# Layer 3 of a four-layer image network: softmax weights used unscaled, their sums made on TensorE, the division on VectorE

## The chip, the cores and the metric

The kernel runs on one core of one Trainium2 chip, as one program for four layers. The metric is the device time in microseconds (us). Three runs of the kernel before gave 3361.9, 3371.34 and 3377.48 us; their median is 3371.34 us.

## The reference, cut to what matters

The input is a batch of 8 images of 32 x 32 tokens with 256 channels. Each of the four layers adds its output to its input. Only layer 3 changes, a windowed attention with 8 heads of 32 channels and a window of 7 x 7 tokens:

```
qkv  = silu(x @ w_qkv.T)                       # q, k get an RMS norm and a scale per head; v does not
wp   = silu(x @ w_wp.T + b_wp)                 # gives width and sharp, one each per token and head
scores = einsum('blhd,blwhd->blhw', q, k_win) * D ** -0.5
soft = sigmoid((width - rel_dist) * sharp)
scores = scores - (1 - soft) * 10000.0
attn = softmax(scores)                         # over the 49 places of the window
out  = einsum('blhw,blwhd->blhd', attn, v_win)
out  = rms_norm(out, w_on)                     # over the 256 channels of a token
return silu((out + v) @ w_out.T)
```

The softmax divides each row of exponentials by its sum. The division can be made on the weights, before they meet the values, or on the weighted sum of the values, which is what the change moves.

## The kernel before, in words

A layer is a block in which each engine has its own program, written out by hand; engines meet at semaphores (`wait_ge`, `then_inc`). No planner orders anything: what stands in the loops is the order on each engine, and each engine takes its instructions strictly in that order.

An image is cut into 64 tiles of 4 x 4 tokens. The keys of a tile are the 10 x 10 tokens around it. A step N handles 4 tiles, so 16 steps make an image and 128 steps the layer; in the text a step's number n within its image runs from 0 to 15, and b is the image. In a tile 16 tokens x 8 heads fill the 128 partitions, and 100 keys lie along the row, so a step's weights are 128 x 400 numbers (`logits`).

The work of one step, in class `Tiles`:

- TensorE `scores` (L1762, with a mask added by L1754), for steps N and N + 1 together when N is even.
- VectorE `add_and_low` (L1802): adds the soft mask, and takes the least value of a row, for both steps at the even one.
- ScalarE `exps` (L1822): four activations of 128 x 100, each with its own row's least value as bias, each followed by a read of its accumulated sum.
- VectorE `invert` (L1808): the reciprocal of the 128 x 4 sums, one step later.
- GpSimd `scale` (L1829): multiplies 128 x 400 weights by these, one step later.
- TensorE `turn` (L1774): transposes the weights, two steps after the scores.
- VectorE `copy_turned` (L1814): copies them out of PSUM.
- TensorE `weigh` (L1789): 32 small matmuls (4 tiles x 8 heads), three steps after the scores. Each fills 32 partitions by 16 columns, so four lie side by side in the array. Each matmul of fp32 data in the code is two in the trace.

The weighted sums of 8 steps (half an image) gather in two PSUM banks; `copy_out` on ScalarE (L2679, at n = 10 and at n = 2 of the next image) takes them to `OT` and squares them (L2682). TensorE averages the squares (`out_mean`, L2409, after the other work of n = 11 and of n = 3), ScalarE makes the root (`root_of_out`, L2690, L2692), VectorE scales (`finish`, L2519, L2522), and the output projection (L301 with `w_out`) follows.

Beside this, the steps of image b also prepare image b + 1: projections at n = 4 to 10 (L2366, L309, L301, L2349), each read by ScalarE's tanh (L2617) and VectorE's product (L2494) through a ring of two PSUM banks (`ring`), so that a projection waits until the one two places before it has been taken; squares, means and roots of queries and keys at n = 10 to 15 (L2641, L2643, L2391, L2657, L2659), and VectorE's scaling of queries and keys by them (L2531, L2512). The scores of the next image wait for the last scaled key. GpSimd makes the soft mask's arguments at n = 4 to 10 (`soft_args`, L2786), ScalarE its tanh (`soften`, L2627). The group norm of the next image takes VectorE (L386 to L395), TensorE (L400), GpSimd and ScalarE at n = 0 to 3.

Of the kernel before, what the change touches and what calls it, by code (L numbers as in the profile page):

```python
# [13 lines left out]
P = 128  # L14
# [1827 lines left out]

def edge(t):
    return 0 if t == 0 else 2 if t == BANDS - 1 else 1
# [352 lines left out]
def layer3_order():  # L2197

    order = [("gn", 0)] + [unit_name(u, -1) for n in range(4, 11) for u in layer3_units(n) if u[0] != "out"]
    order += [("mean", 0, j) for j in range(8)]  # L2200
    for b in range(B + 1):
        for n in range(STEPS):
            if b < B:
                order += {0: [("vT", b, 0, 0)], 1: [("vT", b, 0, 1), ("vT", b, 1, 0)], 2: [("vT", b, 1, 1)]}.get(n, [])
            if n == 2 and b + 1 < B:
                order.append(("gn", b + 1))
            order += [name for name in (unit_name(u, b) for u in layer3_units(n)) if name is not None]
            if b + 1 < B:
                order += [("mean", b + 1, j) for j in range(*MEANS_AT.get(n, (0, 0)))]
            if n == 3 and b > 0:  # L2210
                order.append(("om", b - 1, 1))
            if n == 11 and b < B:
                order.append(("om", b, 0))
    return order


def layer3(nc, A, x, out, vimg):
    with ExitStack() as ctx:
# [29 lines left out]
        OT = L.sb("OT", [P, HALVES, T])  # L2248
# [8 lines left out]
        w = Tiles(L, keys, IMAGE, vimg, 5)  # L2257
# [16 lines left out]
        with nc.Block() as block:  # L2274
# [66 lines left out]
            def _(pe):  # L2341
# [12 lines left out]
                def unit(name):  # L2354
# [21 lines left out]
                    elif kind == "k":  # L2376
                        g, half = name[2] % 2, name[2] // 2
                        pe.wait_ge(xn_ready, 4 * (b + 1))
                        ring.may_fill(pe, name)
                        project(nc, ring.region(name), wqkv, xn, HALVES + g, half * BANK, (half + 1) * BANK).then_inc(ring.filled(name), 1)  # L2380
                    else:
                        half, m = name[2], name[3]
                        pe.wait_ge(z_ready, 4 * b + 2 * half + 2)
                        ring.may_fill(pe, name)
                        project(nc, ring.region(name), wo, OT, m, half * BANK, (half + 1) * BANK).then_inc(ring.filled(name), 1)
# [36 lines left out]
                for N in range(B * STEPS + 10):  # L2422
# [19 lines left out]
                    if 3 <= N < B * STEPS + 3:  # L2442
                        w.weigh(nc, pe, N - 3)
                    for u in layer3_units(n):
                        if unit_name(u, b) is not None:
                            unit(unit_name(u, b))
# [3 lines left out]
                    if n == 3 and b > 0:  # L2450
                        out_mean(b - 1, 1)
                    if n == 11 and b < B:
                        out_mean(b, 0)

            @block.vector
            def _(dve):
# [57 lines left out]

                def finish(b, half, g):
                    s = slice(half * BANK, (half + 1) * BANK)
                    H = 2 * b + half
                    dve.wait_ge(or_ready, H + 1)
                    vstep(dve, nc.vector.scalar_tensor_tensor(OT[:, g, s], OT[:, g, s], w_on[:, g:g + 1], orec[:, :], ALU.mult,  # L2519
                                                              ALU.mult))  # L2520
                    ring.is_taken(dve, ("vT", b, half, g))
                    nc.vector.tensor_tensor(OT[:, g, s], OT[:, g, s], VT[:, H % 3, g, :], ALU.add).then_inc(z_ready, 1)  # L2522
# [18 lines left out]
                nc.vector.memset(all_mean[:, :], 1.0 / C)  # L2541
                nc.vector.memset(keys[0][:, :, :], 0.0)
# [23 lines left out]
                for N in range(B * STEPS + 10):  # L2566
# [30 lines left out]
                    if n == 12 and b < B:  # L2597
# [4 lines left out]
            def _(act):  # L2602
# [66 lines left out]
                def copy_out(b, half):  # L2669
                    H = 2 * b + half  # L2670
                    act.wait_ge(w.weighed, STEPS // 2 * (H + 1))
# [4 lines left out]
                    s = slice(half * BANK, (half + 1) * BANK)  # L2676
                    for g in range(HALVES):
                        bank = PS[:, (4 + g) * BANK:(5 + g) * BANK]
                        nc.scalar.activation(OT[:, g, s], bank, ACT.Copy).then_inc(w.o_copied, 1)  # L2679
                    for g in range(HALVES):  # L2680
                        act.wait_ge(w.o_copied, 2 * H + g + 1)
                        nc.scalar.activation(osq[:, g, :], OT[:, g, s], ACT.Square).then_inc(o_squared, 1)  # L2682
# [42 lines left out]
                for N in range(B * STEPS + 10):  # L2725
                    b, n = step_of(N)
                    if n == 4:
                        nc.scalar.preload_act_table_set("exp_and_others")
# [11 lines left out]
                    if n == 2 and b > 0:  # L2740
                        copy_out(b - 1, 1)
                    if n == 2 and b + 1 < B:
                        norm.root(nc, act, b + 1)
                    if n == 3 and b > 0:
                        root_of_out(b - 1, 1)
# [6 lines left out]
                    if n == 10 and b < B:  # L2752
                        copy_out(b, 0)
# [4 lines left out]
                    if n == 11 and b < B:  # L2758
# [10 lines left out]
            def _(pool):  # L2769
# [124 lines left out]
```

## Time and profile before

| | |
|---|---|
| median of three runs | 3371.34 us |
| the profiled execution | 3381.97 us |
| its span in the profile | 3380.1 us |
| its granted TensorE clock, mean | 0.946 |
| layer 3, first exponentials to the end | about 2660 to 3380 us |

The profile is of one execution. A row of a group of instructions has how often it ran, its busy time, the mean of one, and the idle time of its engine ahead of it with what ended it. A row of the order in time has start, length, engine, line and operation. Successive operations of one engine overlap by a little, so that a chain of them is measured from start to start. Line numbers are those of the kernel before.

### The profile page before, as it was taken

The numbers are of one execution on the slowest core, as the hardware profiler recorded it, in microseconds if no ns is written. First come the engines' busy times: TensorE is split into PE (matmuls) and PEld (weight loads), VectorE is DVE, ScalarE is ACT, GpSimd is POOL, SyncE is SP. The second block draws the span as 40 slices with busy tenths as digits, with TensorE's granted clock in tenths as the row PEclk, the third lists the DMA queues.
The fourth block names the chain that finished last, engine by engine and source line by source line (L and its number), as shares of the span: only waits on it lengthen the run. The fifth ranks groups of instructions, "written<-read, shape, count | busy, mean of one in ns | idle before, by whom it ended". The sixth has DMA issues, their size and how long they took to land. (4 is left out here: it accounts for less than half of the span.)

```text
span 3380.1 us, 103119 instructions
## 1 busy us (share of the span) xinstructions
PE 3018.3 (89%) x43264; PEld 1668.5 (49%) x43264; DVE 2138.1 (63%) x5157; ACT 1995.5 (59%) x4348; POOL 1134.3 (34%) x1444
## 2 busy tenths in 40 slices
PE   6999999999985899999999977999995788888886
PEld 2333333333322565555565645667663555555553
DVE  5787778878753676767667643554553466665654
ACT  2667676766662556455556533555552677777774
POOL 3443433434311221222222201222221455554643
PEclk9999999999986999999999988999996899999997
DMA  6877778687763233333333214545444233333332
GB/s 200 163 170 153 172 171 179 143 187 162 145 142 114 62 86 81 73 89 86 86 69 81 67 47 148 159 150 169 149 148 145 69 92 115 117 115 113 117 103 76
DMA packets 299756, 414.89 MB, mean 123 GB/s; under 512 B 39424, under 2 KB 256288, under 8 KB 278304
## 3 DMA queue, kind: packets, MB, share of 16 engines
q1 hardware_dynamic: 275664, 272.46, 27.1%
q0 software_dynamic: 18432, 134.23, 19.9%
q8 instruction: 344, 5.64, 0.7%
q10 hardware_dynamic: 5200, 1.62, 0.2%
q14 instruction: 116, 0.95, 0.1%
HBM read 219.67 MB, written 53.81 MB: 81 GB/s over the span
## 5 line engine op out<-in xcount | busy, mean ns | idle before, releaser
L734 DVE TENSOR_TENSOR l_probs<-l_psum,l_decay 128x1024 f32<-128x1024 f32 x512 | 598.6, 1219 | 164.7 <-PE l_psum L630 154.0
L782 ACT ACTIVATE l_sizes<-l_probs 128x2048 f32<-128x2048 f32 x256 | 487.1, 1908 | 303.2 <-DVE l_probs L734 292.1
L1822 ACT ACTIVATE l_logits<-l_logits,l_low 128x100 f32<-128x100 f32 x1024 | 372.7, 366 | 203.4 <-DVE l_low L1802 202.7
L1829 POOL TENSOR_TENSOR l_logits<-l_logits,l_inv 128x400 f32<-128x400 f32 x256 | 242.9, 950 | 679.9 <-DVE l_inv L1808 679.2
L630 PE MATMUL l_psum<-l_qk 32*128 32x512 f32 x2048 | 340.2, 645 | 7.9 <-POOL l_qk L868 4.2
L883 POOL DMA_DIRECT2D l_sizes<-l_sizes x128 | 111.5, 871 | 549.3 <-ACT l_sizes L782 537.3
L1645 POOL TENSOR_TENSOR l_E<-l_E,l_causal 128x1024 f32<-128x1024 f32 x64 | 153.0, 2390 | 381.6 <-DVE l_x_act L1343 224.6
L645 PE MATMUL l_psum<-l_probs,l_V 128*32 128x512 f32 x2048 | 270.6, 600 | 1.7 <-DVE l_probs L734 1.6
L1814 DVE COPY l_PT<-l_psum 100x512 f32<-100x512 f32 x256 | 173.0, 676 | 114.4 <-PE l_psum L1774 113.9
L301 PE MATMUL l_psum<-l_xT,l_w_up 128*128 128x512 f32 x512 | 231.3, 606 | 9.1 <-DVE l_row_var L1401 9.0
L1789 PE MATMUL l_psum<-l_PT,l_V_windows 100*32 100x16 f32 x16384 | 202.6, 187 | 34.9 <-issue 22.6
L2786 POOL TENSOR_SCALAR l_soft<-l_dist,l_sharp,l_border 128x100 f32<-128x100 f32 x512 | 225.4, 459 | 0.1
L630 PEld LDWEIGHTS l_psum<-l_qk 32*128 32x128 f32 x2048 | 100.7, 184 | 248.8 <-issue 190.3
L1789 PEld LDWEIGHTS l_psum<-l_PT,l_V_windows 100*32 100x32 f32 x16384 | 174.3, 112 | 87.0 <-issue 84.2
L1774 PE MATMUL l_psum<-l_ident,l_logits 128*100 128x128 f32 x1024 | 166.2, 287 | 33.4 <-POOL l_logits L1829 30.5
L1822 ACT ACTIVATION_READ_ACCUMULATOR l_logits<-l_logits,l_low 128x1 f32 x1024 | 191.9, 187 | 0.0
L1774 PEld LDWEIGHTS l_psum<-l_ident,l_logits 128*100 128x100 f32 x1024 | 118.1, 134 | 103.3 <-POOL l_logits L1829 50.1
L301 PEld LDWEIGHTS l_psum<-l_xT,l_w_up 128*128 128x128 f32 x512 | 97.0, 195 | 121.1 <-issue 121.1
L1500 ACT ACTIVATE l_E<-l_E,l_tok_vals 128x128 f32<-128x128 f32 x512 | 155.9, 393 | 0.0
L1802 DVE CUSTOM_DVE_ANT_0 l_logits<-l_psum,l_soft 128x100 f32<-128x100 f32 x512 | 98.5, 256 | 86.5 <-issue 67.0
L1762 PE MATMUL l_psum<-l_keys,l_q_blocks 64*32 64x100 f32 x8192 | 141.4, 259 | 10.4 <-issue 8.1
L654 PE MATMUL l_psum<-l_sizes,l_ones 128*32 128x512 f32 x1024 | 137.5, 609 | 11.8 <-DMA l_sizes<-l_sizes 11.8
(246 smaller groups left out, 5883.8 us busy)
## 6 DMA issues: line engine op xcount, KB each, us to landing
l_sizes<-l_sizes POOLq DMA_DIRECT2D x128, 1024.0 KB, 7.6
l_V_windows<-v_image SPq DMA_DIRECT2D x512, 100.0 KB
l_V_windows<-v_padded SPq DMA_DIRECT2D x512, 100.0 KB
l_E<-rows_c SPq DMA_DIRECT2D x64, 512.0 KB, 5.8
l_xT<-y SPq DMA_DIRECT2D x24, 1024.0 KB, 5.3
y<-l_res SPq DMA_DIRECT2D x32, 512.0 KB, 3.1
l_e_everywhere<-rows_e SPq DMA_DIRECT2D x112, 128.0 KB, 5.6
l_xT<-x SPq DMA_DIRECT2D x8, 1024.0 KB, 11.3
```

Of the source, the lines that this page charges most:

```text
L301: i = nc.tensor.matmul(out, w[:, k, m * P:(m + 1) * P], act[:, k, n0:n1], start=(k == 0), stop=(k == tiles - 1))
L630: i = nc.tensor.matmul(out[:, a * BANK:(a + 1) * BANK], qk[r:r + HD, g, 1, J * P:(J + 1) * P], qk[r:r + HD, g, 0, m * BANK:(m + 1) * BANK] ...
L645: i = nc.tensor.matmul(PS[a * HD:(a + 1) * HD, 6 * BANK:7 * BANK], V[:, J, h * HD:(h + 1) * HD], probs[:, N % 2, a, :], start=(J == 0), st ...
L734: nc.vector.tensor_tensor(probs[:, N % 2, 2 * p:2 * p + 2, :], ring.region(name).rearrange("p (a n) -> p a n", a=2), decay[:, h:h + 2, s0: ...
L782: nc.scalar.activation(sizes[:, slot(N), :, :], probs[:, N % 2, :, :], ACT.Abs).then_inc(sized, 1)
L1500: i = nc.scalar.activation(E[:, N % 3, h, :], E[:, N % 3, h, :], ACT.Exp, scale=-1.0, bias=vals[:, u % 2, c0:c0 + 1])
L1774: m = nc.tensor.transpose(self.ps[0:NKEY, c0:c0 + P], self.logits[:, N % 4, i, :], self.ident[:, :])
L1789: m = nc.tensor.matmul(out[:, r0:r0 + TILE, tc * TILE:(tc + 1) * TILE], self.v[0:NKEY, N % self.slots, i, h * HD:(h + 1) * HD], self.pt[0: ...
L1814: nc.vector.tensor_copy(self.pt[0:NKEY, N % 2, :], self.ps[0:NKEY, (2 + N % 2) * BANK:(3 + N % 2) * BANK]).then_inc(self.pt_ready, 1)
L1822: nc.scalar.activation(e, e, ACT.Exp, scale=-1.0, bias=self.low[:, N % 4, i:i + 1], accum_out=self.total[:, N % 4, i:i + 1]).then_inc(self ...
L1829: nc.gpsimd.tensor_tensor(p, p, self.inv[:, N % 4, :].unsqueeze(2).to_broadcast([P, STEP, NKEY]), ALU.mult).then_inc(self.p_ready, 1)
L2786: m = nc.gpsimd.tensor_scalar(soft[:, M % SOFTS, i * NKEY:(i + 1) * NKEY], dist[:, :], sharp[:, b % 2, t:t + 1], border[:, b % 2, t:t + 1] ...
```

## The change

Layer 3 uses a subclass of `Tiles`, `SummedTiles`. GpSimd now subtracts the least value from the scores ahead of the exponential (`lower`), ScalarE makes one activation of 128 x 400 instead of four with sums (`exps`), and nothing is scaled. TensorE turns and weighs the bare exponentials, and behind the 32 matmuls of a step makes 8 more with a weight of ones, 64 columns each, which give the row's sums in the place of the weighted values. VectorE divides (`divide`) for two steps at a time, at odd steps: a reciprocal of 128 x 256 from PSUM and a product of 128 x 256. The two banks are used by turns of two steps. `OT` has two buffers.

Moved with it: the average of the output's squares (`out_mean`) from behind the work of n = 3 and 11 to the middle of n = 4 and 12; `out_squares`, which is `copy_out` without the copies, by one step; the root of the first half from n = 11 to 12, that of the second half from n = 3 to the head of n = 4; `finish` of the first half from n = 12 to 13. Layer 2 stays as it was.

```diff
+class SummedTiles(Tiles):
+    def bank(self, R):
+        return (4 + R % 2) * BANK
+
+    def weigh(self, nc, pe, N):
+        R = N // 2
+        pe.wait_ge(self.pt_ready, N + 1)
...
+        if N % 2 == 0 and R >= 2:
+            pe.wait_ge(self.o_copied, R - 1)
...
+        for g in range(HALVES):
+            for a in range(4):
+                p = self.place(N, 4 * g + a)
...
+                m = nc.tensor.matmul(out[:, N % 2 * STEP:(N % 2 + 1) * STEP], self.ones[0:NKEY, :], of[:, :, p],
+                                     start=True, stop=True)
+        m.then_inc(self.weighed, 1)
+
+    def exps(self, nc, act, N):
+        act.wait_ge(self.lowered, N + 1)
+        p = self.logits[:, N % 4, :, :]
+        nc.scalar.activation(p, p, ACT.Exp, scale=-1.0).then_inc(self.p_ready, 1)
+
+    def lower(self, nc, pool, N):
+        pool.wait_ge(self.l_ready, STEP * (N + 1))
+        p = self.logits[:, N % 4, :, :]
+        nc.gpsimd.tensor_tensor(p, p, self.low[:, N % 4, :].unsqueeze(2).to_broadcast([P, STEP, NKEY]),
+                                ALU.subtract).then_inc(self.lowered, 1)
...
+                def divide(R):
+                    c0 = w.bank(R)
+                    s = slice(R % 8 * P, (R % 8 + 1) * P)
+                    dve.wait_ge(w.weighed, 2 * (R + 1))
...
+                    vstep(dve, nc.vector.reciprocal(w.share[:, R % 2, :], PS[:, c0 + 2 * P:c0 + 4 * P]))
+                    nc.vector.tensor_tensor(OT[R // 8 % 2][:, :, s], PS[:, c0:c0 + 2 * P].rearrange("p (g t) -> p g t", g=HALVES),
+                                            w.share[:, R % 2, :].rearrange("p (g t) -> p g t", g=HALVES), ALU.mult).then_inc(w.o_copied, 1)
...
-                    if 1 <= N < B * STEPS + 1:
-                        w.invert(nc, dve, N - 1)
                     if 2 <= N < B * STEPS + 2:
                         w.copy_turned(nc, dve, N - 2)
+                    if n % 2 == 1 and 4 < N < B * STEPS + 5:
+                        divide(N // 2 - 2)
...
-                    if n == 12 and b < B:
+                    if n == 13 and b < B:
                         finish(b, 0, 0)
                         finish(b, 0, 1)
...
-                for N in range(B * STEPS + 1):
+                for N in range(B * STEPS):
                     b, n = step_of(N)
-                    if N > 0:
-                        w.scale(nc, pool, N - 1)
+                    w.lower(nc, pool, N)
```

The change moves instructions on four engines. Two places of it follow, of the kernel before and of the changed kernel apart; names begin with `l_`, `ISA` is `add_and_low`, and the line numbers of the changed kernel are its own.

TensorE around n = 11 and 12 before, from the turn of n = 11 to that of n = 13 (`l_O_square` are the squares of the output, `l_square` those of queries and keys):

```order
 L1774 MATMUL l_psum<-l_ident,l_logits 100x128 x4
 L1789 MATMUL l_psum<-l_PT,l_V_windows 32x4x4 x32
 L2409 MATMUL l_psum<-l_O_square,l_all_mean 128x512 x2
 L1754 MATMUL l_psum<-l_outside,l_pick 32x400 x8
 L1762 MATMUL l_psum<-l_keys,l_q_blocks 32x100 x32
 L1774 MATMUL l_psum<-l_ident,l_logits 100x128 x4
 L1789 MATMUL l_psum<-l_PT,l_V_windows 32x4x4 x32
 L2391 MATMUL l_psum<-l_square,l_head_mean 128x512 x2
 L1774 MATMUL l_psum<-l_ident,l_logits 100x128 x4
```

The same stretch of TensorE in the changed kernel:

```order
 L1774 MATMUL l_psum<-l_ident,l_logits 100x128 x4
 L1868 MATMUL l_psum<-l_PT,l_V_windows 32x4x4 x32
 L1876 MATMUL l_psum<-l_PT,l_ones 32x4x4x4 x8
 L1754 MATMUL l_psum<-l_outside,l_pick 32x400 x8
 L1762 MATMUL l_psum<-l_keys,l_q_blocks 32x100 x32
 L1774 MATMUL l_psum<-l_ident,l_logits 100x128 x4
 L1868 MATMUL l_psum<-l_PT,l_V_windows 32x4x4 x32
 L1876 MATMUL l_psum<-l_PT,l_ones 32x4x4x4 x8
 L2460 MATMUL l_psum<-l_O_square,l_all_mean 128x512 x2
 L2442 MATMUL l_psum<-l_square,l_head_mean 128x512 x2
 L1774 MATMUL l_psum<-l_ident,l_logits 100x128 x4
```

The average of the output's squares moved behind the scores of n = 12 and 13 and directly ahead of the means, and each weighing has 8 sums behind it.

VectorE from the end of n = 12 to the first scores of n = 14 before (`l_O_rec` is the root for the output, `l_q_blocks` the scaled queries):

```order
 L1808 RECIPROCAL l_inv<-l_total 128x4
 L1814 COPY l_PT<-l_psum 100x512
 L2519 SCALAR_TENSOR_TENSOR l_OT<-l_OT,l_w_on,l_O_rec 128x512
 L2522 TENSOR_TENSOR l_OT<-l_OT,l_VT 128x512
 L2519 SCALAR_TENSOR_TENSOR l_OT<-l_OT,l_w_on,l_O_rec 128x512
 L2522 TENSOR_TENSOR l_OT<-l_OT,l_VT 128x512
 L1808 RECIPROCAL l_inv<-l_total 128x4
 L1814 COPY l_PT<-l_psum 100x512
 L2531 SCALAR_TENSOR_TENSOR l_q_blocks<-l_silu_q,l_pair,l_rec 128x32x16 x2
 L1802 ISA l_logits,l_low<-l_psum,l_soft 128x100
```

The same stretch of VectorE in the changed kernel:

```order
 L1814 COPY l_PT<-l_psum 100x512 x2
 L2572 RECIPROCAL l_share<-l_psum 128x256
 L2573 TENSOR_TENSOR l_OT<-l_psum,l_share 128x2x128
 L2592 SCALAR_TENSOR_TENSOR l_q_blocks<-l_silu_q,l_pair,l_rec 128x32x16 x2
 L2581 SCALAR_TENSOR_TENSOR l_OT<-l_OT,l_w_on,l_O_rec 128x512
 L2583 TENSOR_TENSOR l_OT<-l_OT,l_VT 128x512
 L2581 SCALAR_TENSOR_TENSOR l_OT<-l_OT,l_w_on,l_O_rec 128x512
 L2583 TENSOR_TENSOR l_OT<-l_OT,l_VT 128x512
 L1802 ISA l_logits,l_low<-l_psum,l_soft 128x100
```

The four operations of `finish` moved from ahead of the copy of n = 13 to behind the queries of that step, and a division of two steps stands between that copy and the queries; the small reciprocals are gone.

## Rows read from the trace of the kernel before

**Rows 1.** Image 2, n to 10, then 11 on: length; PE, PEld, DVE, ACT, POOL busy; clock.
```profile
2829.20:2893.20 64.00, 57.68 (x1393) 40.80 (x1394) 39.79 (x161) 42.23 (x142) 41.66 (x85) 0.97 0.37 105
2893.20:2917.90 24.70, 19.44 (x507) 10.54 (x505) 15.67 (x55) 24.14 (x67) 6.68 (x6) 1.00 0.43 134
```

**Rows 2.** Chain of waits, image 2: start, length, engine and line.
```profile
2857.61 5.84 POOL l_soft L2786 x12
...
2894.01 1.08 ACT l_OT L2679 x2
...
2902.55 1.54 ACT l_logits L1822 x8
```

**Rows 3.** TensorE in order of time, image 2.
```profile
2838.37 0.28 PE L400 MATMUL l_psum<-l_gn_mean_var,l_group_mean 128*128 128x4 f32 x2
...
2842.16 0.72 PE L1789 MATMUL l_psum<-l_PT,l_V_windows 100*32 100x16 f32 x64 [0.70 <-ACT l_OT L2679]
2843.11 3.64 PE L2409 MATMUL l_psum<-l_O_square,l_all_mean 128*128 128x512 f32 x4 [0.22 <-ACT l_O_square L2682]
...
2848.96 0.75 PE L2366 MATMUL l_psum<-l_xn,l_w_wp 128*32 128x64 f32 x36
2850.93 0.64 PE L2366 MATMUL l_psum<-l_xn,l_w_wp 128*32 128x64 f32 x28 [1.22 <-issue]
...
2866.81 1.95 PE L301 MATMUL l_psum<-l_OT,l_w_out 128*128 128x512 f32 x4 [1.05 <-DVE l_V L2494]
```

**Rows 4.** Groups by line, 2655 to 3350 us.
```profile
L1822 ACT ACTIVATE l_logits<-l_logits,l_low 128x100 f32<-128x100 f32 x512 | 185.8, 365 | 21.9 <-DVE l_low L1802 21.4 <-issue 0.3
L1829 POOL TENSOR_TENSOR l_logits<-l_logits,l_inv 128x400 f32<-128x400 f32 x128 | 133.6, 1045 | 306.5 <-DVE l_inv L1808 305.9
L2627 ACT ACTIVATE l_soft<-l_soft 128x400 f32<-128x400 f32 x122 | 62.4, 534 | 61.8 <-POOL l_soft L2786 61.3
L2366 PE MATMUL l_psum<-l_xn,l_w_wp 128*32 128x64 f32 x448 | 9.5, 224 | 9.5 <-issue 9.5
```

**Rows 5.** VectorE, whole span, groups by line and shape.
```profile
L734 DVE TENSOR_TENSOR l_probs<-l_psum,l_decay 128x1024 f32<-128x1024 f32 x512 | 598.6, 1219 | 164.7 <-PE l_psum L630 154.0 <-ACT l_sizes L782 10.3
L1808 DVE RECIPROCAL l_inv<-l_total 128x4 f32<-128x4 f32 x256 | 44.0, 172 | 4.4 <-ACT l_logits L1822 4.4
L1396 DVE TENSOR_TENSOR l_row_norm<-l_psum,l_row_norm 128x128 f32<-128x128 f32 x64 | 18.7, 292 | 2.2
L1366 DVE COPY l_carry<-l_row_m 128x1 f32<-128x1 f32 x16 | 2.5, 154 | 0.6
```

**Rows 6.** VectorE in order of time, image 2.
```profile
2837.60 0.16 DVE L395 TENSOR_TENSOR l_gn_mean_var<-l_gn_mean_var,l_gn_mean 128x2 f32<-128x2 f32 x1
...
2894.14 0.69 DVE L2494 SCALAR_TENSOR_TENSOR l_silu_q<-l_tanh,l_psum 128x512 f32<-128x512 f32 x1 [1.10 <-ACT l_tanh L2617]
...
2902.14 0.75 DVE L2519 SCALAR_TENSOR_TENSOR l_OT<-l_OT,l_w_on,l_O_rec 128x512 f32<-128x512 f32 x1 [0.17 <-ACT l_O_rec L2692]
...
2904.31 0.69 DVE L2522 TENSOR_TENSOR l_OT<-l_OT,l_VT 128x512 f32<-128x512 f32 x1
...
2905.01 0.66 DVE L1814 COPY l_PT<-l_psum 100x512 f32<-100x512 f32 x1
2905.90 1.41 DVE L2531 SCALAR_TENSOR_TENSOR l_q_blocks<-l_silu_q,l_pair,l_rec 128x512 f32<-128x512 f32 x2 [0.23 <-ACT l_rec L2659]
2908.87 0.26 DVE L1802 CUSTOM_DVE_ANT_0 l_logits<-l_psum,l_soft 128x100 f32<-128x100 f32 x1 [1.55 <-issue]
...
2910.33 0.17 DVE L1808 RECIPROCAL l_inv<-l_total 128x4 f32<-128x4 f32 x1
...
2917.11 0.75 DVE L2512 SCALAR_TENSOR_TENSOR l_keys<-l_keys,l_w_qk,l_rec 128x512 f32<-128x512 f32 x1 [0.49 <-ACT l_rec L2659]
```

**Rows 7.** TensorE in order of time, last image.
```profile
3288.84 3.75 PE L2409 MATMUL l_psum<-l_O_square,l_all_mean 128*128 128x512 f32 x4 [0.97 <-issue]
...
3298.55 1.09 PE L1774 MATMUL l_psum<-l_ident,l_logits 128*100 128x128 f32 x4 [3.13 <-POOL l_logits L1829]
```

More of the change, by code:

```diff
@@ L1840, in gather, with __init__ @@
             sp.dma_start(self.v[0:NKEY, N % self.slots, i, :], src).then_inc(self.v_loaded[N % self.slots], 16)
+class SummedTiles(Tiles):
+    def __init__(self, L, keys, side, vimg, slots):
+        Tiles.__init__(self, L, keys, side, vimg, slots)
+        self.ones = L.sb("ones", [P, 32])
+        self.share = L.sb("share", [P, 2, 2 * P])
+        self.lowered = self.inv_ready
+    def bank(self, R):
[3 more added lines that the diff above has]
+        pe.wait_ge(self.pt_ready, N + 1)
+        pe.wait_ge(self.v_loaded[N % self.slots], 16 * STEP * (N // self.slots + 1))
+        if N % 2 == 0 and R >= 2:
+            pe.wait_ge(self.o_copied, R - 1)
+        c0 = self.bank(R)
+        for i in range(STEP):
+            tc = N % 2 * STEP + i
+            for g in range(HALVES):
+                for a in range(4):
+                    h = 4 * g + a
+                    out = self.ps[a * HD:(a + 1) * HD, c0 + g * P:c0 + (g + 1) * P].rearrange("p (r c) -> p r c", c=SIDE)
+                    nc.tensor.matmul(out[:, :, tc * TILE:(tc + 1) * TILE], self.v[0:NKEY, N % self.slots, i, h * HD:(h + 1) * HD],
+                                     self.pt[0:NKEY, N % 2, i * P + self.place(N, h) * 16:i * P + (self.place(N, h) + 1) * 16],
+                                     start=True, stop=True)
+        for g in range(HALVES):
+            for a in range(4):
+                p = self.place(N, 4 * g + a)
+                out = self.ps[a * HD:(a + 1) * HD, c0 + (2 + g) * P:c0 + (3 + g) * P].rearrange("p (r t c) -> p t r c", r=TILE, c=TILE)
+                of = self.pt[0:NKEY, N % 2, :].rearrange("p (i h r c) -> p i h r c", i=STEP, h=NH, c=TILE)
+                m = nc.tensor.matmul(out[:, N % 2 * STEP:(N % 2 + 1) * STEP], self.ones[0:NKEY, :], of[:, :, p],
+                                     start=True, stop=True)
+        m.then_inc(self.weighed, 1)
[8 more added lines that the diff above has]
+                                ALU.subtract).then_inc(self.lowered, 1)
@@ L2206, in layer3_order @@
                 order.append(("gn", b + 1))
+            if n == 4 and b > 0:
+                order.append(("om", b - 1, 1))
+            if n == 12 and b < B:
+                order.append(("om", b, 0))
             order += [name for name in (unit_name(u, b) for u in layer3_units(n)) if name is not None]
@@ L2247, in layer3 @@
         VT = L.sb("VT", [P, 3, HALVES, BANK])
-        OT = L.sb("OT", [P, HALVES, T])
+        OT = [L.sb(f"OT{s}", [P, HALVES, T]) for s in range(2)]
         osq = L.sb("O_square", [P, HALVES, BANK])
@@ L2256, in layer3 @@
         norm = Groups(L, xT)
-        w = Tiles(L, keys, IMAGE, vimg, 5)
+        w = SummedTiles(L, keys, IMAGE, vimg, 5)
         wp_in = square[:, 0:2, 0:P]
@@ L2675, in copy_out @@
                         ring.is_full(act, ("om", (H - 1) // 2, (H - 1) % 2))
-                    s = slice(half * BANK, (half + 1) * BANK)
                     for g in range(HALVES):
[L2678 to L2682, printed above, removed]
+                        nc.scalar.activation(osq[:, g, :], OT[b % 2][:, g, half * BANK:(half + 1) * BANK],
+                                             ACT.Square).then_inc(o_squared, 1)
                 def root_of_out(b, half):
```

41 lines of the change are left out of this document (20 added, 21 removed).

## The prediction, made before the changed kernel had run

> **What bounds the kernel now.** I read the stretches first, then the chain of waits, then TensorE and VectorE in order of time. Image 2 stands for the six images with work of a neighbour on both sides. It takes 88.7 us from its scores to those of image 3, in two parts with different limits [rows 1]. In n = 0 to 10 TensorE is busy for 57.7 of 64.0 us and no other engine for more than 42.2: the projections of the next image run there, and what TensorE is given more is paid in full. In n = 11 to 15 ScalarE is busy for 24.1 of 24.7 us, TensorE for 19.4, VectorE for 15.7. The chain agrees: exponentials, squares and roots of ScalarE end last there, the eight records of a step's exponentials taking 1.54 us each time [rows 2]. GpSimd comes into the chain once an image, at n = 5, where 5.84 us of mask arguments stand behind a scaling that waited for VectorE's small reciprocal [rows 2].
>
> **ScalarE.** Four activations and four reads fall to one activation of 128 x 400. The nearest row is the mask's tanh of that shape, 534 ns [rows 4]. So 1.54 becomes 0.53, 16 times an image, and the two copies of half an image (1.08 [rows 2]) go twice. That is 16.2 + 2.2 = 18.4 us of ScalarE an image, 5 x 1.01 + 1.08 = 6.1 of it in n = 11 to 15. None of it is time of the kernel unless nothing else is late, and that is where VectorE comes in.
>
> **TensorE.** Eight sums a step are 16 records of 64 columns on 32 columns of the array. The row of that shape is the width and sharpness projection: 36 records in 0.75 us and 28 in 0.64, or 22 ns each with four side by side [rows 3]; 16 x 22 = 0.35 us a step. Bounds: 0.72 us for 64 records of 16 columns [rows 3] give 0.18; records that don't overlap at all, 16 x 224 ns [rows 4], give 3.6. I take 0.35, since shape and columns are the same. In n = 0 to 10 that is 11 x 0.35 = +3.9 us an image.
> Against it stand waits of TensorE in the same part [rows 3]. The weighing of step 0 waited 0.70 us for the copy out of the banks; two banks by turns take that away. The output's mean waited 0.22 for its squares, and took 3.64 us at the lower clock level (1.2 GHz), where the output projection's four records of the same shape took 1.95 at the higher (2.4 GHz); it now stands behind the scores of n = 4, the stretch has no gap, and I take the higher level: 1.7. The output projection waited 1.05 us behind a projection that ScalarE read late because of GpSimd's arguments; GpSimd's subtraction no longer waits for exponentials and small reciprocals, its arguments start sooner by as much, and that goes. Sum -3.7.
>
> **VectorE.** The 16 small reciprocals leave (0.17 us, some 0.09 from start to start). Eight times an image a division comes, at odd steps: a reciprocal of 128 x 256 and a product. The product is an ordinary operation: from 292 ns at 128 to 1219 at 1024 elements it grows by 1.03 ns an element, so 256 take 0.42 us [rows 5]. The reciprocal has one row, 172 ns for 4 elements, and its price an element hides in 172 minus a fixed part. If it streams like the product, 0.42 us: the lower bound. If all 172 ns belonged to the 4 elements, 43 ns each, it would be 11 us: the upper. Between: one element of a copy takes 154 ns [rows 5], so three more cost 18, 6 ns each; 256 take 0.15 + 1.54 = 1.7 us. With 134 ns as the fixed part (a PSUM copy of 512 in 0.66 us, less 512 x 1.03 [rows 6]) it is 9.5 ns each, 2.6 us. I take 1.7, from the row that differs by the fewest elements, and so d = 2.1 us a division; both ends stay for the range.
> The Trainium skill speaks against this change here: "VectorE: DVE Perf Modes", section "First, the fixed hardware budget", says that the reciprocal is an iterative divide with a repeat count of 8. Read as eight cycles an element at the page's 0.96 GHz that is an estimate of 2.3 us, and the sum below would come to some 3400. No row here has a reciprocal of more than 4 elements, so the trace neither shows nor refutes it.
>
> Where d lies. In n = 0 to 10 VectorE has room (39.8 of 64.0 us [rows 1]), and the projections' ring holds a product that is 2 us late. One place has little: at n = 1 the division stands ahead of the group norm's statistics, and TensorE's group mean now starts 0.6 us after their last operation has ended at 2837.76 [rows 3, 6]. TensorE itself comes there 0.7 us later (two steps' sums); VectorE comes 0.35 - 0.1 + 2.1 = 2.35 later, and with some 0.1 for the semaphore the wait is about +1.1. So n = 0 to 10 changes by 3.9 - 3.7 + 1.1 = +1.3.
>
> In n = 11 to 15 the order is what counts. From X, the end of the projections (2893.2): VectorE's last product starts at X + 0.94 [rows 6] and holds it to 1.55, copy 2.15, division 4.25; ScalarE squares two (1.1) to 5.35; TensorE, free from 4.4 (turn, weighing with sums, scores, turn, weighing), makes the output's mean and the first two means of queries, 1.9 each, then the turn of n = 11: X + 9.75. Only then can VectorE copy step 11, and from there it doesn't rest: copy 0.6, division 2.1, queries 1.3, the four operations of `finish` 2.8 (2902.14 to 2904.92), scores of n = 14 and 15 1.46 (2908.87 to 2910.33), copy 0.6, queries 1.3, one key 0.7, copy 0.6, division 2.1, three keys 2.2 [rows 6] = 15.8. The last key is done at X + 25.5. Before it started at 2917.11 and ended at X + 24.7: +0.8. So ScalarE's 6.1 us go to VectorE, which takes ScalarE's place.
>
> New waits. ScalarE's exponential waits for GpSimd's subtraction (0.85 us undisturbed; mean 1.05 with disturbed ones in [rows 4]) behind the mask's arguments of the step before; behind it stand the tanh of that step's projections. GpSimd is busy for 41.7 of 64 us, so I cost it at nothing; at even steps the exponential is ready 1.3 us after the first score instead of 0.3, while the ring's slack is a whole projection (1.95 [rows 3]). The weights are wanted only two steps later. VectorE's wait for the weighing is met, since the copy ahead of it waits for a later turn. The root of the second half now stands ahead of the exponential of n = 4 and waits for a mean in that step; it ended there before too. No DMA is moved.
>
> **The sum.** An inner image +1.3 + 0.8 = +2.1, six of them +12.6. Image 0 has the sums and divisions but no output of a neighbour whose waits go: +3. In the last image the output's mean (3.75 us at the lower clock) moves behind the scores of n = 4 and 5, and the turn that waited 3.13 us for GpSimd's scaling is free of it [rows 7]: -4 after the divisions. The tail has a division for two copies: +0.5. Together +12 on the profiled execution's 3382 us, 3394. That execution lies 10.6 us above the median of the runs; on the median the sum is 3383 us.
>
> **Rivals.**
> 1. The reciprocal streams (0.42 us, d = 0.85). The group mean then waits for nothing, n = 0 to 10 gives 3.9 - 3.7 = +0.2; the squares are done at X + 4.1, so TensorE's 4.4 decides, the turn ends at 8.8, VectorE's 15.8 fall to 13.3: X + 22.1, -2.6. Six images by -2.4, image 0 -1, the last -5: -20, 3351 us. For it: 172 ns for 4 is near the 154 of any small operation [rows 5].
> 2. The reciprocal is dear (9.5 ns, d = 3.0). The group mean waits 2.0, n = 0 to 10 gives +2.2; the squares are done at X + 6.25, the turn at 10.65, VectorE's chain is 17.6: X + 28.2, +3.5. Six by +5.7, image 0 +5, the last -3: +36, 3407 us. It makes the kernel slower from d = 2.4 on or so. The page's eight cycles would be a little less than this.
> 3. TensorE's sums are dear: the small matmuls already stop for 0.7 to 1.2 us with no releaser (1.22 in [rows 3]), and the change adds a seventh to TensorE's records. At 0.9 us a step instead of 0.35, 11 x 0.55 = 6 more an image, 8 images 48: 3430 us.
> That ScalarE gains nothing is not a rival but part of the forecast.
>
> **How the numbers follow.** Forecast 0.38, rival 1 0.32, rival 2 0.23, rival 3 0.07. A measurement of this kernel can tell about 0.5% from no change, that is 3354 to 3388. Errors of 2 us an image give each case some 12 us either way. Forecast (its own range 3368 to 3400): same 0.25, slower 0.13. Rival 1: faster 0.19, same 0.13. Rival 2: slower 0.20, same 0.03. Rival 3: slower 0.07. So faster 0.19, same 0.41, slower 0.40. The range 3342 to 3418 reaches into both main rivals and leaves out about 0.07 below and 0.11 above. A reciprocal at its upper bound of 11 us would be far outside.
>
> **What would show it.** The reciprocal's mean: 1.7 right, 0.4 rival 1, over 2.3 rival 2. The sums: 16 records within 0.35 us behind a weighing. In n = 11 to 15 VectorE should have no rest from the copy of step 11 to the last key, with ScalarE idle ahead of the exponential of n = 14. In n = 0 to 10 the three waits of [rows 3] should be gone, the mean of n = 4 at the higher clock level, and the group mean should wait for VectorE by about 1 us. Wrong would be: ScalarE still without rest at n = 12 to 15, TensorE's ring waiting for VectorE's products at n = 5 to 9, or GpSimd late with the subtraction at n = 5 to 7.

## The result, and the profile after

The changed kernel takes 3437.49 us in the median (3430.66 to 3446.47), the kernel before 3374.41 beside it: ratio 1.019, 95% interval 1.0146 to 1.0234. It is slower, by 1.5 to 2.3%, and lies 54 us above the forecast, beyond its range.

All traces of this study are read by one cut: the six images 1 to 6, from the first mask record of an image to the end of its last query projection (part A, n = 0 to 10) and from there to the next image (part B, n = 11 to 15). Before, A is 64.5 and B 24.5 us in the mean; after, 70.7 and 27.9. (The rows of image 2 end A 0.3 us earlier, where that projection's last record starts.) So an image is 9.6 us longer instead of 2.1, 57 us over six images; image 0 is 0.4 shorter (83.2 for 83.6), last image and tail 3.2 (102.0 for 105.2). Ahead of layer 3's first scores the code is the same, yet they start between 2650 and 2687 us in the profiled executions here (2658 before, 2669 after), and nothing here explains that; so the cut is sharper than the totals. Each kernel has one trace, though: how far A and B differ between executions of one kernel was not measured, and the six A of a trace lie 1 to 6 us apart.

Image 2 after, A and B (columns as in [rows 1]):

```profile
2850.00:2919.94 69.94, 62.34 (x1569) 44.30 (x1570) 49.18 (x160) 28.54 (x57) 44.54 (x86) 0.95 0.33 94
2919.94:2952.27 32.33, 22.61 (x587) 12.89 (x585) 21.01 (x56) 20.23 (x35) 5.61 (x5) 0.89 0.34 107
```

ScalarE fell from 42.2 to 28.5 and from 24.1 to 20.2 us: 17.6 an image where 18.4 were foretold, but 3.9 of it in B instead of 6.1, since one more pair of roots falls into B. In B no engine is busy for more than 22.6 of 32.3 us: there the time is waiting. The groups of layer 3 after, by line (busy, mean ns | idle before them):

```profile
L1890 POOL TENSOR_TENSOR l_logits<-l_logits,l_low 128x400 f32<-128x400 f32 x128 | 124.0, 977 | 352.0 <-DVE l_low L1802 351.4
L2572 DVE RECIPROCAL l_share<-l_psum 128x256 f32<-128x256 f32 x64 | 111.7, 1746 | 0.0
...
L1884 ACT ACTIVATE l_logits<-l_logits 128x400 f32<-128x400 f32 x128 | 68.0, 532 | 182.5 <-POOL l_logits L1890 182.4
L1876 PE MATMUL l_psum<-l_PT,l_ones 100*32 100x64 f32 x2048 | 64.6, 230 | 20.9 <-issue 20.9
...
L2573 DVE TENSOR_TENSOR l_OT<-l_psum,l_share 128x256 f32<-128x256 f32 x64 | 27.2, 425 | 2.2
```

Three of these durations came as foretold: the reciprocal 1.75 us, its product 0.42, the exponential 0.53 [rows 4, 5]. The two idle times were not: ScalarE waits 182 us for GpSimd's subtraction, and TensorE stops 20.9 us among the sums with no releaser. TensorE in order of time, image 2 (idle time before a row in brackets):

```profile
2861.05 0.39 PE L400 MATMUL l_psum<-l_gn_mean_var,l_group_mean 128*128 128x4 f32 x2 [0.93 <-DVE l_gn_mean_var L395]
...
2869.10 1.98 PE L2460 MATMUL l_psum<-l_O_square,l_all_mean 128*128 128x512 f32 x4
...
2887.64 1.98 PE L301 MATMUL l_psum<-l_OT,l_w_out 128*128 128x512 f32 x4
...
2900.68 3.75 PE L301 MATMUL l_psum<-l_OT,l_w_out 128*128 128x512 f32 x4 [2.84 <-DVE l_silu_q L2545]
...
2925.47 0.31 PE L1876 MATMUL l_psum<-l_PT,l_ones 100*32 100x64 f32 x4
2929.75 0.64 PE L1876 MATMUL l_psum<-l_PT,l_ones 100*32 100x64 f32 x12 [3.97 <-issue]
2930.32 3.78 PE L2460 MATMUL l_psum<-l_O_square,l_all_mean 128*128 128x512 f32 x4
...
2935.91 0.60 PE L1774 MATMUL l_psum<-l_ident,l_logits 128*100 128x128 f32 x4
```

Against [rows 3]: the group mean waits, as foretold; the mean of n = 4 is at the higher clock level (1.98 for 3.64), as foretold. Of the four output projections of an image the second, which had waited 1.05 us, waits no longer, as foretold. But the third waits 2.84 us and then runs at the lower level (1.2 GHz, 3.75 us). Before, it was this row:

```profile
2876.91 1.95 PE L301 MATMUL l_psum<-l_OT,l_w_out 128*128 128x512 f32 x4 [0.17 <-DVE l_silu_q L2494]
```

Over six images the wait of the second fell from 1.1 to 0, that of the third rose from 0.2 to 2.2, and all four together rose from 1.6 to 2.7 us an image; only in image 2 did the third run at the lower level. And in the middle of one weighing's sums TensorE stands for 3.97 us; the mean of n = 12 behind it runs at the lower level, 3.78, and the turn of n = 11, on which VectorE's chain hangs, starts at X + 16.0 (X = 2919.94) instead of X + 9.15 (the prediction's X + 9.75, less the turn's 0.6). VectorE meanwhile:

```profile
2936.55 0.69 DVE L1814 COPY l_PT<-l_psum 100x512 f32<-100x512 f32 x1 [10.14 <-PE l_psum L1774]
...
2950.14 2.07 DVE L2563 SCALAR_TENSOR_TENSOR l_keys<-l_keys,l_w_qk,l_rec 128x512 f32<-128x512 f32 x3
```

From that copy to the last key it takes 15.66 us, foretold 15.8, with no rest but 10 us of idleness ahead of it.

**The stop.** A stop is here idle time of TensorE that no releaser ends. TensorE's loads from one stop to the next:

```profile
2923.29 0.72 PEld L1762 LDWEIGHTS l_psum<-l_keys,l_q_blocks 64*32 64x32 f32 x55 [1.50 <-issue]
2924.16 0.39 PEld L1774 LDWEIGHTS l_psum<-l_ident,l_logits 128*100 128x100 f32 x4 [0.15 <-issue]
2924.74 0.83 PEld L1868 LDWEIGHTS l_psum<-l_PT,l_V_windows 100*32 100x32 f32 x64 [0.18 <-issue]
2925.47 0.15 PEld L1876 LDWEIGHTS l_psum<-l_PT,l_ones 100*32 100x32 f32 x4
2929.75 0.40 PEld L1876 LDWEIGHTS l_psum<-l_PT,l_ones 100*32 100x32 f32 x12 [4.13 <-issue]
```

127 loads, as many matmuls and two waits: 256 records. Counted through the whole trace, nearly all long stops stand a multiple of 256 TensorE records apart (48 of the 57 over 0.7 us; before, 28 of 30). In the same 4 us the DMA queues show:

```profile
q1 hardware_dynamic: 530, 1.02, 64.9%
q8 instruction: 1, 0.02, 1.4%
```

One 16 KB packet of the queue "instruction" (it ran from 2927.36 to 2928.30), beside 1 MB of other transfers; TensorE went on 1.45 us after it. Of the stops at such a multiple every one over 0.7 us in the six images ends 1.2 to 1.6 us after such a packet. There are 103 such packets in the six images, and TensorE's 26,250 records are 102.5 times 256; before, 91 for 90.5. So TensorE waits for its program. In six images these stops are 41.3 us after and 16.0 before.
The Trainium skill ("Runtime: NRT & Kernel Launch", section "Instruction fetch mechanics") says that instructions come in 16 KiB blocks of 256 while the engine runs, the crossing mostly hidden. The trace agrees on the block; hidden it is not here, with 6.9 us an image.

**GpSimd.** GpSimd, then ScalarE, ahead of the third output projection:

```profile
2889.58 4.25 POOL L2844 TENSOR_SCALAR l_soft<-l_dist,l_sharp,l_border 128x100 f32<-128x100 f32 x8
2896.85 0.24 POOL L2832 TENSOR_SCALAR l_sharp<-l_args 128x64 f32<-128x64 f32 x1 [3.02 <-DMA l_args<-l_rec]
...
2897.90 0.85 POOL L1890 TENSOR_TENSOR l_logits<-l_logits,l_low 128x400 f32<-128x400 f32 x1
```

```profile
2898.79 0.54 ACT L1884 ACTIVATE l_logits<-l_logits 128x400 f32<-128x400 f32 x1 [4.38 <-POOL l_logits L1890]
2899.23 1.06 ACT L2679 ACTIVATE l_tanh<-l_psum 128x512 f32<-128x512 f32 x2
```

At n = 7 GpSimd waits for the DMA with the next image's width and sharpness. Before, a scaling stood behind that wait, wanted a step later:

```profile
2874.91 0.24 POOL L2774 TENSOR_SCALAR l_sharp<-l_args 128x64 f32<-128x64 f32 x1 [1.66 <-DMA l_args<-l_rec]
...
2875.98 0.86 POOL L1829 TENSOR_TENSOR l_logits<-l_logits,l_inv 128x400 f32<-128x400 f32 x1
```

Now the subtraction of n = 8 stands there, behind it the exponential, the tanh, VectorE's product, the projections' ring and TensorE.

### The profile page after: what moved, and what is told of

Same layout as the page of the kernel before. It is cut to its first block and busy times, and to the rows that moved or that the text cites. A ratio compares the mean times of both kernels' runs of the same rounds, so it can differ in the third digit from the quotient of the medians.

```text
span 3444.7 us, 106350 instructions
## 1 busy us (share of the span) xinstructions
PE 3053.7 (89%) x45312; PEld 1703.4 (49%) x45312; DVE 2255.3 (65%) x5158; ACT 1855.1 (54%) x3420; POOL 1132.6 (33%) x1444
## 5 line engine op out<-in xcount | busy, mean ns | idle before, releaser
L1822 ACT ACTIVATE l_logits<-l_logits,l_low 128x100 f32<-128x100 f32 x512 | 186.9, 366 | 182.9 <-DVE l_low L1802 182.8
L1890 POOL TENSOR_TENSOR l_logits<-l_logits,l_low 128x400 f32<-128x400 f32 x128 | 124.0, 977 | 352.0 <-DVE l_low L1802 351.4
L1829 POOL TENSOR_TENSOR l_logits<-l_logits,l_inv 128x400 f32<-128x400 f32 x128 | 109.1, 853 | 381.5 <-DVE l_inv L1808 379.1
L1884 ACT ACTIVATE l_logits<-l_logits 128x400 f32<-128x400 f32 x128 | 68.0, 532 | 182.5 <-POOL l_logits L1890 182.4
L1802 DVE CUSTOM_DVE_ANT_0 l_logits<-l_psum,l_bias 128x100 f32<-128x100 f32 x512 | 102.7, 257 | 71.3 <-PE l_psum L1762 71.3
L1387 DVE TENSOR_TENSOR l_faded<-l_state,l_tok_vals 128x264 f32<-128x264 f32 x48 | 37.2, 774 | 162.6 <-PE l_psum L1265 162.6
```

What stands on the lines that cost most here:

```text
L1822: nc.scalar.activation(e, e, ACT.Exp, scale=-1.0, bias=self.low[:, N % 4, i:i + 1], accum_out=self.total[:, N % 4, i:i + 1]).then_inc(self ...
L1890: nc.gpsimd.tensor_tensor(p, p, self.low[:, N % 4, :].unsqueeze(2).to_broadcast([P, STEP, NKEY]), ALU.subtract).then_inc(self.lowered, 1)
```

## The experiments

Times are medians, ratios go to the kernel before of the same runs; A and B are means over the six images of one trace. The traced execution lies up to 22 us above its kernel's median (run 3) and up to 18 us below it (run 1).

| kernel | median, ratio (interval) | A | B | A + B |
|---|---|---|---|---|
| before | 3374.4 to 3388.2 | 64.5 | 24.5 | 88.9 |
| changed | 3437.5, 1.019 (1.0146 to 1.0234) | 70.7 | 27.9 | 98.5 |
| 1 arguments behind step 8 | 3438.5, 1.0167 (1.0127 to 1.0206) | 67.9 | 28.1 | 96.1 |
| 2 sums in half as many | 3414.7, 1.0091 (1.0058 to 1.0124) | 67.8 | 25.8 | 93.6 |
| 3 no sums | 3423.0, 1.0122 (1.0076 to 1.0168) | 69.2 | 26.2 | 95.4 |
| 4 copy for reciprocal | 3412.2, 1.0083 (1.0053 to 1.0112) | 70.4 | 26.1 | 96.6 |
| 5 = 1 + 2 | 3393.0, 1.0036 (1.0009 to 1.0064) | 66.2 | 25.8 | 92.0 |
| 6 divisions moved | 3432.0, 1.0115 (1.0076 to 1.0154) | 69.4 | 27.6 | 97.0 |
| 7 all moves | 3401.7, 1.0059 (1.0025 to 1.0092) | 68.8 | 23.7 | 92.5 |
| 8 exponential alone | 3387.2, 1.0002 (0.9974 to 1.003) | 67.3 | 22.1 | 89.4 |
| 9 = 8, arguments moved | 3343.5, 0.9873 (0.9823 to 0.9922) | 62.9 | 21.2 | 84.1 |
| 10 = 7, finish spread | 3406.8, 1.0063 (1.0034 to 1.0092) | 70.2 | 23.7 | 93.9 |
| 11 sums in twice as many | 3470.0, 1.0254 (1.0208 to 1.0299) | 72.6 | 28.5 | 101.2 |
| 12 = 5, copy | 3351.1, 0.9895 (0.9855 to 0.9934) | 64.1 | 22.3 | 86.4 |
| 13 = 9, old division | 3404.0, 1.0085 (1.0053 to 1.0117) | 67.2 | 25.5 | 92.7 |
| 14 = 13, pairs | 3408.2, 1.0087 (1.0061 to 1.0114) | 67.3 | 26.2 | 93.5 |
| 15 = 3, arguments moved | 3400.3, 1.006 (1.0037 to 1.0084) | 65.4 | 26.3 | 91.6 |

**1.** GpSimd's arguments behind the subtraction of step 8.

```diff
                     w.lower(nc, pool, N)
+                    if b + 1 < B and n == 8:
+                        affine(b + 1)
...
-                        if n == 7:
-                            affine(b + 1)
```

> One line moved: GpSimd's three operations on the width and sharpness of the next image (and the wait for the DMA that brings them) stand behind its subtraction of step 8 instead of ahead of it. Theory G (ScalarE's exponential now waits for a GpSimd that stands still for those arguments: 3.0 us at n = 8 of image 2, then TensorE stops 2.7 us ahead of the output projection and runs its next 12 records at the lower clock): each of six images loses that stop, 2 us of it and about as much of low clock, so 3 to 4 us an image, 3415 to 3420 us, and the wait of the exponential of n = 8 falls from 4.4 to about 1 us. Theory I (TensorE stops for its instructions) and theory V (the division on VectorE) expect 3437 within 7.

GpSimd, then TensorE at the third and fourth output projection of image 2:

```profile
2884.61 0.85 POOL L1890 TENSOR_TENSOR l_logits<-l_logits,l_low 128x400 f32<-128x400 f32 x1 [2.09 <-DVE l_low L1802]
2885.43 0.24 POOL L2832 TENSOR_SCALAR l_sharp<-l_args 128x64 f32<-128x64 f32 x1
```

```profile
2887.38 1.96 PE L301 MATMUL l_psum<-l_OT,l_w_out 128*128 128x512 f32 x4
...
2894.87 1.96 PE L301 MATMUL l_psum<-l_OT,l_w_out 128*128 128x512 f32 x4 [0.56 <-DVE l_keys L2545]
```

The subtraction waits for VectorE alone, and the projection runs at once and at the higher level. TensorE's waits at the output projections fall from 2.7 to 0.8 us an image and A falls by 2.7, under the forecast: the exponential of n = 8 still waits 2.4 us in image 2, and the time at the lower clock level in A hardly falls (6.0 to 5.6). The total does not fall (3438.5 for 3437.5 us; the traced executions took 3420 and 3446), so this run alone does not show the price. Runs 2 and 5, 3 and 15, 8 and 9 differ by this edit too, and there the ratio falls: from 1.0091 to 1.0036, from 1.0122 to 1.006 and from 1.0002 to 0.9873.

**2.** Both halves of the heads in one matmul.

```diff
-        for g in range(HALVES):
-            for a in range(4):
-                p = self.place(N, 4 * g + a)
+        for a in range(4):
+            p = self.place(N, a)
...
```

> The sums of both halves of the heads come in one matmul of 128 columns instead of two of 64: 16 records a step fewer of some 312 on TensorE (matmuls and loads together), the same columns, the same result. Theory I (TensorE stops at every 256th record until a 16 KB piece of its program has landed, some 4 us from piece to piece where it runs dry): 16 records are a sixteenth of a piece, 0.25 us a step in the dense steps n = 0 to 3 and 11 to 15, so 2 to 3 us an image, 3418 to 3425 us, with stops at piece ends down from 6.9 to about 5 us an image. If the sums cost only by their columns: no change, 3437 within 7. Theories G and V: no change.

4.9 us an image, more than expected of theory I and against a price by columns. The stops at 256 fall from 41.3 to 19.7 us in six images. In all six images B is 25.8 us. Image 2, B, then VectorE in it:

```profile
2911.02:2936.80 25.78, 19.45 (x545) 10.81 (x543) 20.95 (x56) 20.20 (x35) 5.61 (x4) 1.00 0.43 131
```

```profile
2921.04 0.69 DVE L1814 COPY l_PT<-l_psum 100x512 f32<-100x512 f32 x1 [3.89 <-PE l_psum L1774]
...
2934.63 2.07 DVE L2562 SCALAR_TENSOR_TENSOR l_keys<-l_keys,l_w_qk,l_rec 128x512 f32<-128x512 f32 x3
```

Without a stop the copy of n = 11 starts at X + 10.0 and the last key ends at X + 25.7: the prediction had X + 9.75 and X + 25.5.

**3.** No sums: the loop over them left out, `PS[:, c0:c0 + 2 * P]` under the reciprocal.

> The sums are left out; VectorE's reciprocal reads the weighed values themselves, so the output is not softmax. TensorE has the records of the kernel before again (280 a step). Theory I: stops at piece ends return from 6.9 to 2.7 us an image as in the kernel before, and the sums' own time (0.36 us, 11 steps in which TensorE sets the pace) goes too, 4.2 + 4.0 an image, some 3388 to 3400 us. If the sums cost by their streaming alone (the 0.35 us of the prediction): 3.9 an image, 3412 to 3416. If GpSimd or VectorE set the loss: above 3425.

Only 3.1. The stops fell to 10.2 us in six images, but TensorE's waits at the output projections rose to 3.9 an image and its time at the lower clock level from 9 to 17. The median, 3423 us, lies between the cases. Inconclusive alone; run 15 repeats it without GpSimd's wait.

**4.** `nc.vector.tensor_copy` for `nc.vector.reciprocal`.

> VectorE's reciprocal of 128 x 256 (1.75 us) is a copy of the same shape (some 0.4 us), so the output is not divided. 1.3 us less, eight times an image. Theory V (the division stands on the path in n = 12 to 15 and ahead of the statistics at n = 1): three of the eight count, 3.9 us an image, some 3410 to 3415 us. Theories I and G: the division lies beside other work, under 1 us an image, 3431 to 3437.

The median lies where theory V put it (3410 to 3415). The group mean's wait goes (1.5 to 0.1), and in image 0, with no stop in B, that part is 21.9 us for 25.8: 3.9 less, three reciprocals. But the stops grow to 57.6 us in six images and take back half. So the division does stand on the path, and what one engine gives, the next stop takes.

**5.** Edits 1 and 2 together.

> The edits of the first two runs together: GpSimd's arguments behind the subtraction of step 8, and sums in half as many records. In the traces the first took 2.4 us from each of six images and the second 4.9. If they act on different stops (G at n = 8 and 9, I mostly in n = 11 to 15 and n = 0 to 3) they add: 7.3 an image, some 3393 us, 91.2 us an image. If TensorE merely finds its next stop earlier: no more than the larger, 93 us an image, 3407.

6.6 of 7.3: they add. What is left against the kernel before, 3.0 us an image and a ratio of 1.0036, is about what the prediction forecast (2.1, and 3383 to 3371).

**6.** Three divisions elsewhere on VectorE.

```diff
-                    if n % 2 == 1 and 4 < N < B * STEPS + 5:
+                    if n in (3, 5, 7, 9, 11) and 4 < N < B * STEPS + 5:
...
+                    if n in (1, 14, 15) and 4 < N < B * STEPS + 5:
+                        divide(N // 2 - 3 if n == 14 else N // 2 - 2)
```

> The changed kernel with three of its eight divisions in other places on VectorE and nothing else: that of n = 1 behind the group norm's statistics, that of n = 13 behind the key of n = 14, that of n = 15 behind its three keys. Theory V: from the end of the projections to the next image 25.8 us (undisturbed) less two divisions, 21.5 to 22.5, so 27.9 falls to about 24 in the mean; the wait of the group's mean falls from 1.5 to about 0.2 us; together 5 us an image, some 3407 us. Theory I: TensorE's stops set that part, it stays at 27 to 28, 3430 to 3437.

The group mean's wait is gone, but B stays: the weighings now wait for a bank (2.7 us an image in B). With two banks the division's place isn't free. Theory V's 3407 us is missed.

**7.** On top of runs 5 and 6, the output's first half out of B (`out_squares` at n = 12, `out_mean` and `root_of_out` at n = 14, `finish` at n = 4, a fourth slot of `VT`, two of `orec`), both subtractions of a pair first.

> All of that, and the output's first half out of the last five steps: its squares behind n = 12, its mean behind n = 14, its four operations of VectorE in n = 4 of the next image (with a fourth slot for the turned values and a second one for the root), and both subtractions of a pair of steps ahead of the mask's arguments on GpSimd. If stops for instructions, GpSimd's arguments and VectorE's place are the whole loss: n = 0 to 10 at 65 to 66 us, the rest at 21 to 22, 87 us an image against 88.9 of the kernel before, some 3360 us. If something else holds the images: 91 us an image or more, 3390.

B loses 2.1 us against run 5, A gains 2.6, of it 1.7 at the second values projection, behind `finish`. Missed.

**8.** The exponential alone, in the kernel before: `exps` and `lower` of the change, `invert` and `scale` out.

> The kernel before with one exponential a step behind GpSimd's subtraction and nothing else: no totals, no small reciprocals, no scaling by GpSimd, so the output is not divided; no sums, no division, the old banks and places. ScalarE's last five steps fall from 24.1 us of work to 18, no division comes to VectorE: they should go from 24.5 to 19 to 21 us. Theory G: n = 0 to 10 grows by 1 to 2 us, since the output projection waits for a ScalarE that waits for GpSimd's arguments (1.3 us a wait becomes 2.5); net 2 to 4 us an image faster than before, ratio 0.993 to 0.996. If GpSimd's place costs nothing: 4 to 5 an image, ratio 0.990 to 0.992.

B -2.4, A +2.8: nothing gained, where 2 to 5 us an image were expected. GpSimd and TensorE, image 2:

```profile
2893.09 0.24 POOL L2786 TENSOR_SCALAR l_sharp<-l_args 128x64 f32<-128x64 f32 x1 [3.01 <-DMA l_args<-l_rec]
```

```profile
2896.91 3.75 PE L301 MATMUL l_psum<-l_OT,l_w_out 128*128 128x512 f32 x4 [3.17 <-DVE l_silu_q L2508]
```

The same wait, with neither sums nor division in the kernel.

**9.** Run 8 with edit 1.

> The kernel of the run before with one exponential and no division, and GpSimd's three operations on the next image's arguments behind the subtraction of step 8. Theory G: the wait of the output projection falls from 3.3 to at most 1.3 us an image and the low clock from 8.5 to about 4, so n = 0 to 10 returns from 67.3 to 64 or 65 us; with 22 for the rest 86 to 87 us an image, ratio to before 0.993 or less. If that part is longer for another reason: 67 us and no change.

```profile
2821.93:2887.10 65.17, 58.99 (x1396) 42.31 (x1397) 39.67 (x150) 30.80 (x61) 43.52 (x86) 0.95 0.34 98
2887.10:2907.88 20.78, 18.66 (x505) 10.86 (x504) 15.53 (x50) 20.42 (x36) 6.61 (x4) 1.00 0.53 173
```

5.2 us an image from moving three small operations (A and B of image 2, as above); the output projections' waits fall from 3.4 to 0.7. Theory G holds.

**10.** Run 7 with the four calls of `finish` at n = 4, 5, 6 and 7, one each.

> The version with all moves, and the four operations of the output's first half in pairs behind n = 4 and n = 5, those of the second behind n = 6 and n = 7. In its trace TensorE waited 1.6 us at the second values projection, which came with those four operations in n = 4, and 0.7 to 1 us at output projections. If these waits go: 66.5 + 23.7, 90 us an image and some 3385 us, no better than the version with two edits. If VectorE is late all the same: 92.5 us an image as before.

The values projection's wait falls from 1.7 to 0.6, but the output projections' rise from 1.2 to 2.6. Missed.

**11.** Each sum in two matmuls (`for j in range(0, STEP, 2)`).

> The changed kernel with each sum in two matmuls of 32 columns instead of one of 64: 32 records a step more, the same columns, the same result. Theory I: the mirror of the halved sums; 32 records are an eighth of a piece of 256, 0.5 us a step where TensorE runs dry, twice the step from halved to full: 6 to 10 us an image more, some 3475 to 3500 us, stops at piece ends from 6.9 to over 10 us an image. If columns count: 3437 within 10.

Slower, but by 2.7 an image, not 6 to 10; the stops stay at 7.2. No mirror of run 2.

**12.** Run 5 with the copy.

> The version with two edits (arguments behind step 8, sums in half as many records) with a copy in place of the reciprocal, so the output is not divided. What is left of the loss there, 3 us an image against the kernel before, should be the division: TensorE's wait of 1.6 us for the group's mean goes, and the last five steps lose three reciprocals' difference, 25.8 to 21.9 us; 86.5 to 87 us an image, ratio to before 0.993 or less. If the division is not what is left: 91 to 92 us an image, ratio 1.00.

```profile
2815.92:2879.88 63.96, 59.13 (x1484) 41.67 (x1485) 43.24 (x160) 28.75 (x57) 44.01 (x86) 1.00 0.35 102
2879.88:2902.36 22.48, 19.73 (x544) 11.21 (x543) 16.96 (x56) 20.04 (x35) 5.61 (x4) 1.00 0.49 159
```

As expected: what run 5 leaves is the reciprocal.

**13 and 14.** Run 9 with VectorE's `tensor_reduce` over the exponentials, the small reciprocal and GpSimd's scaling; then with both subtractions of a pair first.

> The kernel before with one exponential a step behind GpSimd's subtraction, GpSimd's arguments behind step 8, and the division as before (a small reciprocal and GpSimd's scaling), except that VectorE sums the exponentials itself, one operation of 128 x 400 a step. No sums on TensorE, no division of 128 x 256; the output is the reference's. Without any division this was 84.1 us an image against 88.9 before. Added: some 0.55 + 0.2 us a step on VectorE, five of them in the last steps, and 0.85 on GpSimd. If the loss lay only in the change's way to divide: 85 to 88 us an image, ratio to before 0.990 to 0.998. If one more operation on VectorE and GpSimd stands on the path at every step: 89 to 92, ratio 1.000 to 1.006.

> The same with both subtractions of a pair of steps one behind the other on GpSimd, ahead of the scaling and the mask's arguments. If the exponentials of odd steps wait for GpSimd's arguments (3 to 6 us of them in n = 4 to 9): 1 to 2 us an image less than the run before. If they are ready in time anyhow, or the scaling is late instead: the same within 0.5 us, or up to 1 us more.

Beside one exponential the old way to divide costs 8.6 us an image: TensorE's turns wait 6.3 us an image for the scaled weights. The order of the pair changes little. So the loss does not lie in the change's way to divide alone.

**15.** Run 3 with edit 1.

> The changed kernel without sums (the reciprocal reads the weighed values, so the output is not softmax) and with GpSimd's arguments behind step 8. Beside the version with both edits (8 records of sums a step, 92.0 us an image) and the one with arguments moved alone (16 records' pairs, 96.1): if each record costs the same, half of the sums was worth 4.1 and the other half is too: 88 us an image. If they cost only where TensorE runs dry, the second half is worth less: 90 to 91.

91.6, where half the sums gave 92.0: the second half of the records is nearly free, even if this trace has more time at the lower clock level (12.4 us an image for 7.0). It speaks for a price where TensorE runs dry, not for one by the record, but with one trace and that much more low clock it does not prove it.

## Why the prediction was wrong, point by point

Two steps failed: the price of the sums, which left out TensorE's stops, and the cost of ScalarE's wait for GpSimd, put at nothing. Run 5 takes back 6.6 of the 7.5 us by which an image came out longer than forecast. A third term, the waits that should go, was too large.

- **The reciprocal** (1.7 us, d = 2.1): right, 1.75 and 2.17. The Trainium skill's repeat count of 8 ("VectorE: DVE Perf Modes", "First, the fixed hardware budget") had led to an estimate of 2.3; the measurement is lower.
- **n = 11 to 15, +0.8**: the order was right to 0.2 us and gives +1.3 where nothing stops TensorE (runs 2 and 5); the mean of +3.4 has 2.1 more from stops for instructions and the lower clock behind them.
- **The group mean, +1.1**: right, 0.2 to 1.5, and gone with the copy (run 4).
- **The sums, 0.35 us a step**: this step failed. The records themselves took that, some 0.4 where nothing stopped. The price left out the stops, which rose from 16.0 to 41.3 us in six images: half the records back were worth 4.1 to 4.9 us an image (runs 2 and 5). This is rival 3, given 0.07 and at 3430 us nearly the time that came; but its "0.9 us a step" is not how it works (runs 11 and 15): the stops come once in 256 records.
- **"I cost it at nothing"** (ScalarE's exponential behind GpSimd's subtraction): this step failed. GpSimd's load of 41.7 of 64 us was read, not what stood in its queue: a wait for a DMA ahead of the subtraction. "No DMA is moved" was true, and beside the point, since an urgent operation was moved behind one. The third output projection's wait went from 0.2 to 2.2 us an image. Moving the arguments gives 1.6 to 5.2 us an image back (runs 1, 2 and 5, 3 and 15, 8 and 9).
- **The waits that should go, -3.7**: all went, but three of them had been read from image 2 alone, and over six images they were smaller. The waits for the weighing in A were 0.3 (0.70 foretold) and those for the squares 0.1 (0.22). The mean of n = 4 had run at the higher clock level in three of the six images already, and after the change it does so in four: 2.8 to 2.4 us in the mean, 0.4 instead of 1.7. The second output projection's 1.1 went as foretold. Together 1.9. The time at the lower level in A rose from 3.4 to 6.0 us an image.
- **Image 0 +3, the last -4, the tail +0.5**: -0.4, and -3.2 together.

TensorE in A: idle 6.6 to 9.0 us an image (stops +1.5, output projections +1.1, group mean +1.3, the rest -1.5), busy 57.8 to 61.7. In run 5 the stops are back at 15.9 us in six images, and an image is 3.0 us longer than before, near the forecast's 2.1. That nearness is in part luck: the waits gave less than forecast, and half of the sums' records are gone. Not settled: why a doubling of the sums cost so little more, and what delays the packets; whether the 1 MB of window transfers beside the packet does it was not tested. No version that divides beat the kernel before.

## What to carry to other kernels

An operation put ahead of a busy engine brings its own engine's queue with it: look for every wait that stands before it there, DMAs first, not for that engine's load. Count an engine's instructions as well as their columns where it runs hundreds of small ones, and look whether its stops without a releaser stand at equal counts. Take the waits that a change is to remove from all repetitions, not from one.

## What was not expected of the hardware

TensorE stops at multiples of 256 records, up to 3.97 us, until 1.2 to 1.6 us after a 16 KB packet has landed; halving the 16 matmul records of a step's sums more than halved these stops (41.3 to 19.7 us in six images). The reciprocal of 128 x 256 takes 1746 ns where a copy of the same shape takes 413 (run 12).
